# The first value unit of an attention chunk in the first stage: four units behind its scores instead of three

## The reference, cut to what matters

```python
qkv = x @ w_qkv                                   # per head: q, k, v of 64
scores = q @ k.T / 8;  causal mask;  attn = softmax(scores)
x = layernorm(x + (attn @ v) @ w_out)
# ternary weights: w_t = sign(w) * (|w| > 0.5 * mean|w|); input divided by its rms
h = gelu(rmsnorm(x) @ w_up_t.T)
x = layernorm(x + rmsnorm(h) @ w_down_t.T)
```

## Time and profile before

| | |
|---|---|
| median of 3 runs | 2234.31 us (2232.63 to 2281.22) |
| profiled execution, its own time | 2230.4 us |
| its span, slowest core (core 4) | 2228.8 us |
| spans of the eight cores | 2221.4 to 2228.8 us |
| mean granted TensorE clock, core 4 | 0.995 |
| TensorE / VectorE / ScalarE / GpSimd busy | 95% / 57% / 61% / 16% |

### The profile page before, as it was taken

One profiled execution on the slowest core, in us unless ns is written; L12 is line 12 of the kernel. 1 busy time (PEld: TensorE's weight loads), 2 busy tenths in 40 slices (PEclk: granted clock), 3 DMA queues, 4 the chain that ended last, 5 costly groups with the idle time before them and its releaser, 6 DMA issues.

```text
span 2228.8 us, 54671 instructions; the slowest of 8 cores (2221.4 to 2228.8 us)
## 1 busy us (share of the span) xinstructions
PE 2128.0 (95%) x21250; PEld 1310.0 (59%) x21250; DVE 1267.4 (57%) x2292; ACT 1349.0 (61%) x1436; POOL 354.8 (16%) x574
## 2 busy tenths in 40 slices
PE   5999999899999999999999999999999999999998
PEld 2555555555555555566656756656656746657665
DVE  2466666676677674456555645555545535445654
ACT  1588898789888898733344445455565575665111
POOL 4222121222222221201110110011010110100110
PEclk9999999999999999999999999999999999999999
DMA  9236444343434345301101110011010100100100
GB/s 155 65 113 163 134 141 140 91 123 105 123 105 126 96 115 155 124 1 46 51 20 39 39 46 32 21 46 32 20 37 22 39 20 21 51 11 30 39 20 20
DMA packets 77948, 154.72 MB, mean 69 GB/s; under 512 B 27392, under 2 KB 45952, under 8 KB 76672
## 3 DMA queue, kind: packets, MB, share of 16 engines
q1 hardware_dynamic: 70880, 134.44, 18.8%
q0 software_dynamic: 6816, 16.78, 4.8%
HBM read 134.42 MB, written 33.55 MB: 75 GB/s over the span
## 4 chain that ended last, share of the span: by engine, by line
PE 85%; DVE 5%; ACT 5%; issue 3%; DMA 1%; DVEq 0%; POOL 0%; ACTq 0%; POOLq 0%
PE mm L76 61%; PE sc L76 13%; PE pv L76 11%; ACT pb L76 4%; ACT L76 1%; DVE ast L76 1%; DVE kt L76 1%; DMA xT<-xt 1%; DVE nrm L76 1%; DVE vs L76 0%; DVE pb L76 0%; DVE qt L76 0%; DVE yb L76 0%; DVE rec L76 0%; ACT hT L76 0%
## 5 line engine op out<-in xcount | busy, mean ns | idle before, releaser
L76 ACT ACTIVATE pb<-sc,bias 128x1024 bf16<-128x1024 f32 (+3 forms) x1152 | 1160.2, 1042 | 423.9 <-PE sc L76 408.6
L76 PE MATMUL mm<-wdn,hT 128*128 128x512 fp8e4 x2048 | 479.3, 380 | 0.0
L76 PEld LDWEIGHTS pv<-vs,pb 128*128 128x128 bf16 x8448 | 364.0, 98 | 170.7 <-issue 44.1
L76 PE MATMUL pv<-vs,pb 128*128 128x65 bf16 x8448 | 409.0, 194 | 24.7 <-DVE ast L76 17.5
L76 ACT ACTIVATE hT<-mm 128x512 bf16<-128x512 f32 x256 | 152.9, 597 | 343.9 <-PE mm L76 343.3
L76 PEld LDWEIGHTS mm<-wdn,hT 128*128 128x128 bf16 x2048 | 186.7, 98 | 243.6 <-issue 51.6
L76 PE MATMUL mm<-xT,wq 128*128 128x512 bf16 x1024 | 307.3, 390 | 15.1 <-DMA xT<-xt 15.1
L76 PE MATMUL sc<-qt,kt 64*128 64x512 bf16 (+3 forms) x1440 | 269.0, 370 | 2.7 <-ACT pb L76 2.4
L76 PE MATMUL mm<-xnT,wupa 128*128 128x256 bf16 x2048 | 231.1, 273 | 2.3 <-ACT hT L76 1.3
L76 PEld LDWEIGHTS mm<-xnT,wupa 128*128 128x128 fp8e4 x2048 | 198.2, 98 | 28.2 <-issue 4.2
L76 DVE TENSOR_TENSOR hsq<-hT 128x512 f32<-128x512 bf16 x240 | 166.0, 692 | 57.5 <-ACT hT L76 53.0
(11 more groups left out here) (63 smaller groups left out, 1774.2 us busy)
## 6 DMA issues: line engine op xcount, KB each, us to landing
wr<-w_up SPq DMA_DIRECT2D x64, 512.0 KB, 3.8
wr<-w_down SPq DMA_DIRECT2D x64, 512.0 KB, 3.7
yb<-x SPq DMA_DIRECT2D x32, 512.0 KB, 3.3
out<-yb SPq DMA_DIRECT2D x32, 512.0 KB, 2.6
xT<-xt POOLq DMA_DIRECT2D x16, 512.0 KB, 35.9
wq<-w_qkv POOLq DMA_DIRECT2D x24, 256.0 KB, 6.6
att_s<-ast SPq DMA_DIRECT2D x40, 128.0 KB, 3.1
atto<-att_s SPq DMA_DIRECT2D x8, 640.0 KB, 4.3
```

The costliest lines, as they stand in the source:

```text
L76: ins = ops[op](*args, **kw)
```

## The change

`drain` gets a second argument, how many more units a chunk's first unit may be behind. The first stage's call passes 2, the second stage's passes 1, which is the old rule.

```diff
-    def drain(lag):
-        while pend and len(pend) > lag + (pend[0][3] == 0):
+    def drain(lag, more):
+        while pend and len(pend) > lag + more * (pend[0][3] == 0):
             emit_pv()
...
                     side_pull(side_pace * wide)
-                drain(LAG)
+                drain(LAG, 2)
     work.finish()
...
                 work.pull(2 * pace)
-                drain(LAG)
+                drain(LAG, 1)
             work.add(*last)
```

## The result

The changed kernel takes 2219.6 us (median of 6 runs, 2217.9 to 2220.7). Its ratio to the kernel before is 0.9937, with a 95% interval of 0.9924 to 0.9949: faster by 0.6%, some 14 us.

The account below looks back on a forecast made before the run. The prediction took TensorE to set the pace in the first stage. Its terms, 14.4 − 0.2 − 0.3 − 1.5 + 1.7, gave 14.1 us less, 2216 us profiled and 2220 as a median, with a stated range of 2213 to 2233.

Parts of the forecast that it names:

- within 2%: Whole kernel: time changes by no more than 2% either way; chance 0.97.
- likeliest case: Whole kernel: 9 to 19 us gained, own range 2215 to 2226 us; chance 0.68.
- Order on TensorE: First-stage chunk heads: unit 4's scores and projection work move ahead of value units 0 and 1, about 0.77 us.
- The sum of waits: First-stage heads: value matmuls' 18.9 us of waits for VectorE's division fall to 4.5, saving 14.4 us.
- the 1.37 of the prediction: Head with the longest wait, 3.50 us: moved work takes 1.37 us, leaving 2.1 us of wait.
- ScalarE (0.5 us): First-stage heads: unit 4's scores wait for exponential 2, costing 0.2 us at 37 heads and 0.3 at five.
- the 6 that the prediction allowed: First stage, sign to check afterwards: scores wait for ScalarE under 6 us.
- Rival (b): First-stage heads: ScalarE becomes the bound, making the kernel 5.7 us slower, 2240; chance 0.07.
- VectorE (1.5 us, bounds 0 to 5): First stage: TensorE arrives earlier at VectorE's evictions and waits there, costing 1.5 us, bounds nothing to 5.
- rival (a): First-stage heads: VectorE's lateness reappears one step later at evictions, leaving 3 to 9 us gained; chance 0.18.
- the 30 that the prediction allowed: First stage, sign to check afterwards: projection or norm matmuls wait for VectorE under 30 us.
- The clock (+1.7): First stage: of two half-speed stretches, the one at 585 to 588 goes and the other stays, gaining 1.7 us.

Follow-up runs that it names:

- e4: Kernel before, with four units of lag only at the seven heads of four-unit chunks and three at all others; ratio to the kernel before 0.9964.
- e9: Kernel before, with four units of lag at heads of longer chunks and three at the seven heads of four-unit chunks; ratio to the kernel before 0.9983.
- e6: Changed kernel with a lag of five units at the first stage's heads and six pb buffers instead of five; 2218.4 us, ratio to the kernel before 0.9939.
- e11: The changed kernel run once more, nothing edited; 2219.6 us, ratio to the kernel before 0.9939.
- e1: Kernel before, with the first stage's lag at chunk heads cut from three units to two; 2268.8 us, ratio to the kernel before 1.0165.
- e3: Changed kernel with drain called ahead of the side work, so the division precedes it on VectorE; 2218.6 us, ratio to the kernel before 0.9939.
- e7: Changed kernel, but three units of lag where a norm matmul falls due with the next work; 2221.0 us, ratio to the kernel before 0.9948.
- e8: Changed kernel with three units where a norm matmul falls due next, and drain ahead of the side work; ratio to the kernel before 0.9935.

## Why the prediction came out as it did

**The amount.** 2220 was forecast, 2219.6 measured. That it is so near is in part luck. The three runs of the kernel before that the ratio counts have the median 2232.6, which is 2.2 and not 3.9 us above the profiled one, and against it the gain is 13.0 where the sum had 14.1; the two errors cancel. Against its own base, the profiled execution (2230.4 to 2219.8), the gain is 10.6 us on the slowest core and 12.6 on core 4.

| term of the sum | taken | measured |
|---|---|---|
| waits for the division, gone | 14.4 | 16.8 |
| ScalarE | −0.5 | −2.1 |
| VectorE | −1.5 | −4.5 |
| clock | +1.7 | +1.1 to +1.7 |
| together | 14.1 | 11.3 to 11.9 |

The stage is shorter by 12.3 us over the mean of the cores, so the measured terms leave 1 us or less open.

**The direction, and what can be told.** I put 0.97 on "within 2%" and wrote that this is about what a measurement can tell from no change. This step failed: the interval is ±0.13%, and the 0.6% that the sum itself gave stands clear of it. A reader who took "within 2%" for "no difference" was misled; by the text's own likeliest case it was faster by 9 to 19 us, and so it is.

**Order on TensorE.** Right. The groups are of 24, and of 18 in four-unit chunks (not 20 to 22, as the prediction had it; units 0 to 2 have 8, 6 and 4), and all but three come without a wait for the division. e4 and e9 show that the two kinds of heads gain by themselves.

**The sum of waits (14.4 of 18.9, 4.5 left).** In the trace 2.1 us are left. About half of the difference is not a gain: in the four-unit chunks a part of the gap is now spent one step earlier, at the scores. The longest wait shows both pieces, and the clock in the stretches around it:

```profile
410.56 0.39 PE L76 MATMUL sc<-qt,kt 64*128 64x512 bf16 x2 [0.88 <-ACT pb L76]
...
413.18 1.15 PE L76 MATMUL pv<-vs,pb 128*128 128x65 bf16 x18 [1.42 <-DVE ast L76]
```

```profile
408.00:411.00 3.00, 0.94 (x10) 1.00 0.47 178
411.00:415.00 4.00, 2.58 (x31) 0.51 0.16 33
```

3.50 became 0.88 + 1.42, so 1.2 was hidden, near the 1.37 of the prediction.

**ScalarE (0.5 us).** Its waits rose by 2.1 to 6.6, past the 6 that the prediction allowed, and all of it at the short chunks. I had counted these as swallowed by the gaps; with the 2.1 that are left for the division they make 4.2, against the 4.5 + 0.5 that were taken for both. Rival (b), ScalarE as the bound, is refuted by e6: even a lag of five units leaves the score waits at 6.3. That also bears on the rule cited from the Trainium skill (Perfetto Trace Analysis, "Identifying the Most-Contended Engine"): by it ScalarE at 86% would have been the engine to relieve, since TensorE's weight loads are at 55% of the same window, and 14 us were to be had without touching its work. That section names the share of peak flops beside the weight-load share, and that was not worked out here.

**VectorE (1.5 us, bounds 0 to 5).** This is the mis-sized term, the step of the sum that failed, and rival (a) has its place here. On core 4 kt, qt, vs and qst together went from 27.3 us (the earlier trace rows for the first two; vs 5.1, qst 3.2) to 31.1, where 1.9 us more stand under value matmuls that wait for qst, since the record of a norm matmul is missing. Core 1, complete in both kernels, went from 27.4 (11.3, 7.8, 5.1 and 3.2) to 32.3:

```profile
PE mm L76 <- DVE kt L76: 12.3, 21, 1.2
PE mm L76 <- DVE vs L76: 8.9, 16, 1.0
PE mm L76 <- DVE qt L76: 7.7, 10, 3.3
PE mm L76 <- DVE qst L76: 3.4, 6, 1.3
```

The six cores that are complete before have a mean of 27.6, the six that are complete after one of 32.2: 4.5 us came back, three times what I took, and the waits passed the 30 that the prediction allowed. I took the low end because VectorE idles soon behind a head. That idle was the wrong row to look at: what counts is what stands between the division and the next eviction, and whether TensorE's moved work asks for that eviction. At 14 of the 42 heads the moved work held a norm matmul; I saw this as "more work" that lengthens the distance, and at five it was a new wait. With 4.5 for 1.5 alone the sum is 11.1 us, between the 10.6 (slowest core) and the 12.6 (core 4) of the profiled execution.

**The clock (+1.7).** Core 4 has lost the slow stretch at 585 and kept the one behind the longest wait, as taken. It has also lost one near 387 and got one near 172, of 3.4 us each, which nobody forecast and which cancel. Half of TensorE's busy time in these stretches is 5.6 us before and 4.4 after on core 4, and 4.9 and 3.2 over the mean of the cores: 1.2 to 1.7 given back (1.1 in e11). e1 shows the size of this term when waits grow: 11 to 12 of its 35 us.

## What to carry to other kernels

A wait that recurs at a loop's seam can be summed head by head from the timeline, as the smaller of the wait and the work moved ahead of it. As a sum of that wait it held within 2.5 us (47 forecast and 49.5 seen when the lag was cut, 14.4 and 16.8 when it grew); it doesn't say what comes back elsewhere. But when work is moved ahead of a wait, look at what that work itself needs: if it asks for something from the same late engine, the wait moves along, and everything behind it pays. In this kernel the lag's optimum is flat: one unit more, a better-chosen unit, or a better order on the late engine each removed waits from one row of the list and put them into another, and the variants e3, e6, e7 and e8 ended within 0.13% of each other.

## What was not expected of the hardware

Waits of 0.3 to 3.6 us at 38 heads, 1.3 on average, took the mean granted clock of the span from 0.995 to 0.988 (e1); in the stage that cost 11 to 12 us on top of the 30.6 that the waits grew by. No run here isolates how the clock decides: there are more half-speed stretches where there was more idle (on core 4 ten in the stage of e1, three before, one in e6), and still a wait of 1.94 us was followed by full clock.
